# Cross attentions: rotation partners by a VectorE shuffle, and TensorE's other work laid out anew behind the score products

## The reference

```python
H, D = 16, 16
q = (x_q @ W_q).reshape(B, Tq, H, D).transpose(0, 2, 1, 3)
k = (kv[..., :C]).reshape(B, Tkv, H, D).transpose(0, 2, 1, 3)
x1, x2 = x[..., ::2], x[..., 1::2]              # of q, and of k
x1p, x2p = x1 * cos - x2 * sin, x1 * sin + x2 * cos
rotated = jnp.stack((x1p, x2p), axis=-1).reshape(x.shape)
att = jnp.einsum('bhqd,bhkd->bhqk', q, k) / jnp.sqrt(D)
att = jax.nn.softmax(jnp.where(mask, att, -1e9), axis=-1)
y = jnp.einsum('bhqk,bhkd->bhqd', att, v)        # then @ W_c, added to x
```

## Time and profile before

| | |
|---|---|
| median of 3 runs | 2953.72 us (2947.42 to 3137.99) |
| profiled execution, its own time | 2952.82 us |
| its span, first to last instruction | 2951.0 us |
| TensorE matmuls busy | 2658.3 us (90%) |
| VectorE busy | 1945.2 us (66%) |
| ScalarE busy | 1399.1 us (47%) |
| GpSimd busy | 1107.2 us (38%) |
| `cross0` | about 264 to 829 us |
| `cross1` | about 2145 to 2583 us |

### The profile page before, as it was taken

How to read it: one execution, slowest core, us unless ns; L and a number is a source line. 1 busy time by engine, 2 the same in 40 slices (tenths; PEclk the granted TensorE clock), 3 DMA queues, 4 the chain that set the end, 5 groups by cost and what they waited for, 6 DMA issues and landing times. The chain is left out here.

```text
span 2951.0 us, 51682 instructions
## 1 busy us (share of the span) xinstructions
PE 2658.3 (90%) x17628; PEld 1631.8 (55%) x17629; DVE 1945.2 (66%) x3269; ACT 1399.1 (47%) x2199; POOL 1107.2 (38%) x854
## 2 busy tenths in 40 slices
PE   7997899999868899999999999999889999857998
PEld 4775333333235556565656565656544454456997
DVE  4776777877668765657575656666546666574555
ACT  2433466666558653434343434343335555443333
POOL 3233323233036343435343434343443333063333
PEclk9998799999879999999999999999989999958999
DMA  5002222222111000000000000000043232146666
GB/s 163 0 0 63 61 59 61 58 61 58 30 58 44 1 1 1 1 1 1 1 1 1 1 1 1 1 1 1 1 113 81 74 79 69 37 138 230 219 211 195
DMA packets 102982, 160.60 MB, mean 54 GB/s; under 512 B 28349, under 2 KB 63432, under 8 KB 97160
## 3 DMA queue, kind: packets, MB, share of 16 engines
q1 hardware_dynamic: 97784, 147.88, 17.5%
q0 software_dynamic: 3408, 8.46, 0.8%
q10 hardware_dynamic: 1600, 1.61, 0.2%
HBM read 91.79 MB, written 14.96 MB: 36 GB/s over the span
## 5 line engine op out<-in xcount | busy, mean ns | idle before, releaser
L1678 DVE TENSOR_REDUCE self_nmax<-self_SM 128x2 fp32r<-128x1024 f32 x256 | 313.3, 1224 | 211.7 <-PE self_SM L1567 211.7
L1656 ACT ACTIVATE self_PT<-self_ST 128x1024 f32<-128x1024 f32 x256 | 262.9, 1027 | 329.4 <-PE self_ST L1592 329.4
L1723 POOL TENSOR_TENSOR self_U<-self_PT 128x1024 f32<-128x1024 f32 x64 | 153.9, 2405 | 613.5 <-ACT self_PT L1656 613.5
L499 DVE TENSOR_REDUCE cross_nmax<-cross_S 128x2 f32<-128x1024 f32 x256 | 310.7, 1222 | 110.2 <-PE cross_S L347 109.2
L444 ACT ACTIVATE cross_PT<-cross_S 128x1024 f32<-128x1024 f32 x256 | 260.0, 1023 | 123.3 <-PE cross_S L358 121.4
L1726 POOL TENSOR_TENSOR self_U<-self_U,self_PT 128x1024 f32<-128x1024 f32 x128 | 303.4, 2371 | 31.9 <-ACT self_PT L1656 27.0
L1602 PE MATMUL self_W<-self_PT,self_V 128*64 128x512 f32 x1024 | 237.4, 606 | 19.6 <-ACT self_PT L1656 14.6
L1146 DVE TENSOR_REDUCE cross_nmax<-cross_S 128x4 f32<-128x1024 f32 x128 | 156.5, 1223 | 133.4 <-PE cross_S L967 133.3
L1698 DVE RECIPROCAL self_rcp<-self_W 128x512 f32<-128x512 f32 x64 | 214.7, 3354 | 33.8 <-PE self_W L1609 33.1
L1083 ACT ACTIVATE cross_PT<-cross_S 128x1024 f32<-128x1024 f32 x128 | 131.0, 1024 | 127.6 <-PE cross_S L983 127.4
L1602 PEld LDWEIGHTS self_W<-self_PT,self_V 128*64 128x64 f32 x1024 | 72.5, 139 | 161.4 <-issue 123.2
(11 more groups left out here) (450 smaller groups left out, 7002.8 us busy)
## 6 DMA issues: line engine op xcount, KB each, us to landing
moe_staged<-in_L_ffn_W SPq DMA_DIRECT2D x36, 1024.0 KB, 6.1
cross_ks<-cross_parts SPq DMA_DIRECT2D x384, 64.0 KB, 2.3
cross_qs<-cross_parts SPq DMA_DIRECT2D x376, 64.0 KB, 2.3
all_x<-in_L_ffn_W SPq DMA_DIRECT2D x14, 1024.0 KB
all_x<-sorted_rows SPq DMA_DIRECT2D x83, 130.0 KB, 2.1
cross_cT<-in_ctx_T SPq DMA_DIRECT2D x16, 512.0 KB, 4.6
sorted_rows<-all_spare_row SPq DMA_DIRECT2D x1, 5460.0 KB, 23.8
all_x<-in_x SPq DMA_DIRECT2D x8, 512.0 KB, 4.0
```

The costliest lines, as they stand in the source:

```text
L499: dve.tensor_reduce(nmax[:, g % 2, 0:R, n % PER_G], S[:, slot[st], :, :], AX.X, ALU.max, negate=True).then_inc(s_maxed, 1)
L1656: act.activation(PT[:, k, :, :], ST[:, :, :], ACT.Exp).then_inc(exped.sem, 1)
L1678: dve.tensor_reduce(nmax[:, i, 0:P:D], SM[:, :, :], AX.X, ALU.max, negate=True).then_inc(maxed.sem, 1)
L1723: pool.tensor_tensor(U[:, c % 2, :, :], PT[:, 0, :, :], PT[:, 1, :, :], ALU.add).then_inc(added.sem, 1)
```

## The change

In both stages the partner of each row is fetched by VectorE instead of TensorE. `rot` is no longer a TensorE step; on VectorE it is a `stream_shuffle` of `rows` into `rsin` within each group of 32 partitions (partner p ^ 16), a wait for it, and the multiply by the sines in place. For that the partners have to stand 16 partitions apart: `cross1` had that already, and `cross0` gets it by another order of the columns of W_q and W_k (`spread_order(True)`), with cosine and sine tables to match. The turn matrices, their loads and their place in the tables go. Beside that the due times of TensorE's other work change: in `cross0` `v` and `out` stand one part to a unit, `norm`, `stat`, `root` and `htok` come about two units earlier, `mt` 0.7 earlier; in `cross1` the two parts of `v` and of `out` stand in two units instead of one.

```diff
-            at[("stat", b, i)] = o - 47.4 + i
-        at[("root", b, 0)] = o - 42.0
-        at[("htok", b, 0)] = o - 40.0
+            at[("stat", b, i)] = o - 49.4 + i
+        at[("root", b, 0)] = o - 44.0
+        at[("htok", b, 0)] = o - 42.0
-            at[("norm", b, c)] = o - 38.0 + c
+            at[("norm", b, c)] = o - 39.7 + c
-            at[("mt", b, g)] = o + PER_G * g - 4.1
+            at[("mt", b, g)] = o + PER_G * g - 4.8
-        for m, ts in enumerate(((-14.4, -12.8), (1.6, 3.2))):
+        for m, ts in enumerate(((-4.5, -1.5), (3.5, 6.5))):
             for part, t in enumerate(ts):
                 at[("v", b, m, part)] = o + t
-        for m, ts in enumerate(((41.6, 42.0), (43.2, 43.25))):
+        for m, ts in enumerate(((43.5, 46.5), (51.5, 54.5))):
             for part, t in enumerate(ts):
                 at[("out", b, m, part)] = o + t
-    RINGED = ("norm", "qk", "rot", "v", "out", "mt")
+    RINGED = ("norm", "qk", "v", "out", "mt")
...
+        PARTNER = [p ^ 16 for p in range(32)]
...
-                elif kind == "rot":
-                    dst = free_bank(st)
-                    pe.wait_ge(s_act, nth_act[("qk", b, n, KC - 1)])
-                    if b == 0:
-                        pe.wait_ge(s_rot, 48)
-                    pe.matmul(dst, turnm[:, :], rows[:, n % 2, :], start=True, stop=True).then_inc(s_full, 1)
...
                 elif kind == "rot":
                     if b == 0:
-                        dve.wait_ge(s_rot, 48)
-                    dve.wait_ge(s_full, nth_full[st])
+                        dve.wait_ge(s_rot, 32)
+                    dve.wait_ge(s_act, nth_act[("qk", b, n, KC - 1)])
                     before = ("rope", b, n - 2) if n >= 2 else ("rope", b - 1, n + 2)
                     if before in at:
                         roped(dve, *before[1:])
-                    dve.tensor_tensor(rsin[:, n % 2, :], src, sin[:, :], ALU.mult).then_inc(s_dve, 1)
+                    dve.stream_shuffle(rsin[:, n % 2, :], rows[:, n % 2, :], PARTNER).then_inc(s_shuffled, 1)
+                    dve.wait_ge(s_shuffled, nth_rot[st])
+                    dve.tensor_tensor(rsin[:, n % 2, :], rsin[:, n % 2, :], sin[:, :], ALU.mult).then_inc(s_dve, 1)
...
-            for t, d in zip((turnm, sin, cos), rope[::-1]):
+            for t, d in zip((sin, cos), rope[::-1]):
                 sp.dma_start(t[:, :], d).then_inc(s_rot, 16)
...
-        for m, t in enumerate((-13.0, -9.0)):
+        for m, t in enumerate((-13.5, -9.5)):
             for part in range(2):
-                at[("v", b, m, part)] = o + t + 0.4 + 0.3 * part
+                at[("v", b, m, part)] = o + t + part
-        for m, t in enumerate((27.4, 31.4)):
+        for m, t in enumerate((26.5, 30.5)):
             for part in range(2):
-                at[("out", b, m, part)] = o + t + 0.3 * part
+                at[("out", b, m, part)] = o + t + part
...
-def spread_order():
+def spread_order(paired):
...
+    if paired:
+        d = d % (D // 2) * 2 + d // (D // 2)
     return (8 * c + 4 * g + 2 * p + r) * D + d
```

More of the change, by code:

```diff
@@ L227, in spread_attention @@
     nth_dve = counted([st for st in dve_steps if st[0] in dve_kinds])
+    nth_rot = counted([st for st in dve_steps if st[0] == "rot"])
     nth_high = counted([st for st in act_steps if st[0] == "high"])
@@ L273, in spread_attention @@
         s_full, s_act, s_dve = s.sem("full"), s.sem("by_act"), s.sem("by_dve")
+        s_shuffled = s.sem("shuffled")
         s_guarded, s_maxed, s_scored, s_exped, s_valued = (s.sem(n) for n in ("guarded", "maxed", "scored", "exped", "valued"))
@@ L592, in pool_program @@
                     if b == 0:
-                        pool.wait_ge(s_rot, 48)
+                        pool.wait_ge(s_rot, 32)
                     pool.wait_ge(s_act, nth_act[("qk", b, n, KC - 1)])
@@ L778, in finishing @@
         return [st for st in steps if st[0] not in last_part or st[3] == last_part[st[0]]]
-    RINGED = ("norm", "qk", "rot", "v", "out", "mt", "fix")
+    RINGED = ("norm", "qk", "v", "out", "mt", "fix")
     BY_ACT = ("norm", "qk", "v")
@@ L1050, in pe_program @@
                         m.then_inc(s_full, 1)
[L1051 to L1056, removed]
                 elif kind == "v":
@@ L3282, in rotation_tables @@
     f = np.float32
[L3283 to L3290, removed]
     half = D // 2
     d = np.arange(P) % 32 // 2
+    sign = np.where(d < half, -1.0, 1.0)[:, None]
+    w = f(1.0) / f(10000.0) ** (np.arange(1, D + 1, 2, dtype=f) / f(D))
+    ang = np.arange(1, T + 1, dtype=f)[None, :] * w[d % half][:, None]
+    cos0, sin0 = np.cos(ang).astype(f), (np.sin(ang) * sign).astype(f)
     w = f(1.0) / f(10000.0) ** (np.arange(half, dtype=f) / f(half))
     ang = np.arange(T, dtype=f)[None, :] * w[d % half][:, None]
[L3296 to L3300, removed]
+    cos1, sin1 = np.cos(ang).astype(f), (np.sin(ang) * sign).astype(f)
+    return cos0, sin0, cos1, sin1
 def turned_order():
@@ L3368, in laid_out @@
     m["band_table"] = np.concatenate(parts, 1)
-    spread = spread_order()
-    m["L0_xattn_W_q"], m["L0_xattn_W_c"] = a["L0_xattn_W_q"][:, spread], a["L0_xattn_W_c"][turned_order()]
-    m["L0_xattn_W_k"], m["L0_xattn_W_v"] = a["L0_xattn_W_kv"][:, :C][:, spread], a["L0_xattn_W_kv"][:, C:]
+    paired, spread = spread_order(True), spread_order(False)
+    m["L0_xattn_W_q"], m["L0_xattn_W_c"] = a["L0_xattn_W_q"][:, paired], a["L0_xattn_W_c"][turned_order()]
+    m["L0_xattn_W_k"], m["L0_xattn_W_v"] = a["L0_xattn_W_kv"][:, :C][:, paired], a["L0_xattn_W_kv"][:, C:]
     for n in ("gate", "up", "down"):
```

13 lines of the change are left out of this document (7 added, 6 removed).

## The result

| | median, us | to the kernel before, same chip |
|---|---|---|
| before | 2950.6 | |
| changed | 2982.1 (2974.1 to 2986.1) | 1.0095 (1.0074 to 1.0116) |

A forecast was written before the change was run, and what follows sets the result against it. The chain from VectorE's `rot` through GpSimd, `high` and the exponential to TensorE's `max` was taken to bind `cross0`. 2952.8 + 1 + 30 - 1 + 2 - 6 = 2978.8, stated as 2977 us; range 2908 to 3008.

The forecast's parts named there:

- The shuffle: On VectorE, each `rot` gains a shuffle of 0.70 us and 0.05 for the dependent start, together 0.75 us.
- The chain for n = 0: In `cross0`, later `rot` delays `high` and then `max`; TensorE idles 2.7 us where it idled 0.82.
- n = 2: In `cross0`, `max` at 9.45 us against TensorE's arrival at 7.0: idle 2.4 us, counted as +2.1.
- n = 3: In `cross0`, `max` at 7.9 us against TensorE's arrival at 7.0: +0.9 us per batch.
- behind `htok`: In `cross0`, `htok` moves two units ahead and holds ScalarE 2.06 us in a 1.67 us unit: about +0.5 net.
- the bank behind `mt`: In `cross0`, the next `qk` takes the bank `mt` leaves, and VectorE reaches `mt` late: +0.4 us.
- The batch: In `cross0`, TensorE's 4.8 us saved come back as waits: +0.1 us in sum, batch stays at 64.2 us.
- The clock: In `cross0`, nearly every long TensorE wait makes the clock fall: 12 falls x 2.5 us = 30 us.
- cross1: VectorE's reduce holds the stage: 0.06 us gained per four units, 2 us in the stage, less `stat` steps; -1 us.
- 12.2 us for four units, 0.9 idle: Sign of being right in `cross1`: four units in about 12.2 us, TensorE idle 0.9 waiting for the reduce.
- Ramp and tail: The ramp's rotation at half clock and the tail's better filled units save time: -6 us.
- Rival C: The `high` chain does not bind and TensorE's time is won: 2884 us, or 2911 with `cross0` alone; chance 0.14.

The follow-up runs named there:

- e1: The kernel before with the changed kernel's due times, rotation partners still a TensorE product: 1.0007, 2955 us.
- e2: The changed kernel's shuffle with the due times of the kernel before: 1.0032, 2963 us.
- e4: The changed kernel with useless TensorE products, never read, put into two waits per batch of `cross0`: 1.0001, 2955 us.
- e3: The changed kernel with ScalarE's `high` copy two units later in `cross0`: 0.987, 2918 us.
- e6: The changed kernel with rotation, rope and `high` copy one unit later in `cross1`: 1.0099, 2989 us.

## Why the prediction was right

- **The shuffle**, 0.70 + 0.05 taken: 0.717 to 0.752 us, and 0.78 from its start to the multiply's. The estimate from the Trainium skill (VectorE: DVE Perf Modes, the perf-mode tier table), scaled down by columns, was 0.60; the trace is 0.12 to 0.15 longer, and it decides.
- **The chain for n = 0**: 3.36, 8.10 and 9.79 us from the unit's start were predicted, 3.40, 8.14 and 9.83 measured; idle 2.7 predicted, 2.67 measured, and its two terms came out separately in e1 and e2.
- **n = 2**: the end of `rot` 3.7 and `max` at 9.45 were right (3.74 and 9.48), the idle 2.4 was 2.07. The failed part is TensorE's arrival, 7.0 us put, 7.4 measured: the four units took 6.91 us, not 6.67, one of them held up 0.19 us by a reduce.
- **n = 3** +0.9, measured 0.81; behind `htok` +0.5, measured 0.64 in four of the five batches; the bank behind `mt` +0.4, measured 0.34.
- **The batch**: 64.2 without falls, against 57.6 + 6.7 = 64.3 from the measured parts; the terms that missed (n = 2, `htok`, and the work taken, 4.4 us busy) nearly cancel. Of the five batches two, 75.2 and 75.8 us, lie outside the 64 to 70 that was to be the sign of it.
- **The clock** is the term that was mis-sized. 12 falls x 2.5 us = 30 were predicted. 10 of `cross0`'s 13 long waits had one; in the five full batches it was 9 of 10, and they cost 36.5 us, 4.1 each. The price was taken from slow stretches of about 3.4 and 6.8 us; here some lasted 10 to 14 (at 0.50 from 592.7 to 606.0). That their cause is the wait is e4.
- **cross1**: -1 predicted, +3 measured. A full batch gained 0.37 us (0.24 predicted: four groups x 0.06). The step that failed is "too short for a clock fall": true of the full batches at 1.00, not of the first, which took 53.9 us at a clock of 0.91 against 48.6 at 1.00. TensorE waited 1.52 us at 2258.8 and 1.83 us at 2274.1 in it, each with a fall behind it (0.57 from 2258 to 2266, 0.72 from 2274 to 2280), where the kernel before has no wait over 0.82; idle time grew by 3.9 us, so the clock is only part of the 5.3. And the sign "12.2 us for four units, 0.9 idle" does not follow from 49.94 / 4 less 0.06; measured are 12.4 and 0.6.
- **Ramp and tail** -6 predicted (and +2 for both prologues), -10 measured in `cross0`. Added up, 1 + 30 - 1 + 2 - 6 = +26 was predicted and 36.8 - 10.1 + 3.0 + 1.4 = +31 measured. The sum came within 5 us of the time partly by luck: for the five full batches my terms give about +25 (0.1 and two falls of 2.5 each), against +36.8 measured, and the shorter ramp and tail gave part of it back.

Rival C, that the chain does not bind, was priced at 2911 for `cross0` alone. It failed as a description of the change, and is what one number makes of it: e3, 2918.

## What to carry to other kernels

Before moving work off a full engine, find what is queued behind what in program order on the others. Here ScalarE's `high` stood two units too early and held exponentials behind a chain through three engines, and with it in place taking the product from TensorE shortened a batch by 0.3 us in the old layout and by 0.6, falls aside, in the new; moved by two units, the whole change gains 2.2 us a batch, beside the 1.1 of the move itself. A step that waits for another engine's long chain belongs as late as its reader allows, and when it is moved, look at each new neighbour on each queue (e6), since the due time moves the neighbours of three engines.

## What the hardware showed

- A TensorE idle for 1.57 us was followed by a fall to 1.2 GHz in 2 cases of 6, and one idle for 2.04 us in 6 of 6 in one kernel and 4 of 7 in another. I had expected few at 2 us and none below. No single wait of 1.20 us or less had one in the full batches of `cross0` in those kernels, but in another a fall came behind 0.64 and 0.98 us of idle time within 3 us.
- 40 us of useless products made a kernel 27 us faster.
- Taking the third product, 1.03 us, from a unit left two score products of 0.58 us and then 0.70 us of wait: most of it did not come back.
